# The statements of sixteen attention units in another order on four engines

## The chip, the cores and the metric

The kernel runs on one core of one Trainium2 chip. The metric is the device time of one execution in microseconds (us). The kernel before took 1912.51, 1914.97 and 1917.04 us in three runs; the median is 1914.97.

## The reference

For eight images of 256 x 256 and eight texts of 128 tokens the reference computes, in f32:

```
h  = edge image (grey, two Scharr convolutions, absolute values)   [8, 256, 256]
h  = concat(h, embedded bigram hashes of the text @ proj * scale)  [8, 384, 256]
h += block0(layernorm(h))   # LN, 16 heads of 16, rotary, causal softmax, Wo, LN, GELU MLP 256-1024-256, its own residuals
h += ffn(layernorm(h))      # ternary weights, relu, 256-1024-256
h += attn1(layernorm(h))    # 16 heads of 64 on 4 key heads, rotated queries, slopes * distance, causal,
                            # softmax with 1 added to the sum, Wo
h += experts(layernorm(h))  # router, top 2 of 8 experts, 960 slots each, silu(gate) * up, down, scatter add
```

Each image has 384 rows of 256 in three tiles of 128 rows. The weights' signs, the rotated query weights and the routing are computed in the kernel too.

## The kernel before, in words

After a setup there are sixteen attention units, one for each image and attention layer: units 0 to 7 are block0's attention of image u (layer 0), units 8 to 15 attn1's of image u-8 (layer 1). Then come the routing of tokens and the eight experts; the change touches neither.

A unit is made of one attention and of the dense work of other images that runs beside it. `Kind` says which: `s1` (lnA, queries and keys of the next image of layer 0, turned and stacked into high and low parts), `conv` (edges of the image two ahead), `s2` (output projection, MLP and ternary feed-forward of the image before), `s1p` (lnB, queries, keys and values for the next unit of layer 1), `s3` (output projection of layer 1, lnE and the router's logits). The units are U_FIRST, five U_MID0, U_SIX, U_SEVEN, U_EIGHT (the first of layer 1), six U_MID1 and U_LAST. In U_FIRST the `up0_` banks and the slots of `mlp_norm`, `mlp_rows` and `ffn_norm` carry the ternary weights and the rotated query weights instead. Each compute engine has a function `unit` with two lists of calls, one for each layer; the lists are written out by hand and the engine goes through its list strictly in order. The engines meet only in semaphores.

The attention of a unit has sixteen heads n in eight pairs p. TensorE computes `scores(p)` (causal, three row tiles) into banks 0 to 2. VectorE's `mask_max(n)` adds mask or slopes, writes `probs` (four buffers) and the row maxima (about three instructions and three reads). ScalarE's `exps(n)` takes the exponents with their sums. TensorE's `turn(n, 0)` and `turn(n, 1)` transpose half of the probabilities each, into bank 3 and bank 4. `take_turned(n)` copies bank 3 on ScalarE and bank 4 on VectorE. `mix(g)` multiplies four heads (layer 0) or two (layer 1) by the values into bank 5. `invert` (VectorE), `spread` (GpSimd), `divisors` (TensorE) and `take_divisors` (ScalarE) bring the reciprocal sums into columns, and `weigh` (VectorE) multiplies bank 5 with them, which frees it. `scores_ahead`, `mask_ahead` and the calls with `_last` belong to the seam with the next or the previous unit.

All dense products use banks 6 and 7 in turn. `dense_units` lists them in TensorE's order and `psum_plan` gives the k-th of them bank 6 + k % 2; a product waits until the last but one has been taken out of its bank (`banks.wait_free`). So the order of this list and of TensorE's calls must agree, and whoever takes a bank late holds up the second product behind it. A row-tile normalisation is three steps: `moments` on VectorE, `deviation` on GpSimd (the reciprocal root), the normalising instruction on VectorE; then TensorE transposes tile by tile (`lnA`, `lnB`, `lnM`, `lnF`, `lnE`). `rope(t)` on GpSimd rotates the queries and keys of tile t as soon as VectorE has taken them; ScalarE's `stack_upper(0)` waits for all three. SP's queue issues the loads and stores of each unit (text, images, spilled sums, `h_rows`, and after U_EIGHT the weights `wo1`); its order is in its own function and is not changed.

Lines: transposes of probabilities L982, of reciprocals L993, of normalised rows L918, scores L966, values products L1017, all products of `product` L1034, stacking L1056, down of the ternary layer L1194, exponents L1729, masking L2290, `take_turned` L1737 and L2433, normalising L2212, rotation L3165 to L3173.

Of the kernel before, what the change touches and what calls it, by code (L numbers as in the profile page):

```python
# [134 lines left out]
def dense_units(k):  # L135
# [6 lines left out]
    if k.layer == 0:  # L142
        add(k.tail is not None, "rinvT_tail")
        add(True, "v0_0", "v0_1")
        add(k.s2, "proj0_0", "proj0_1")
        add(True, "v0_2")
        add(k.s1, "lnA0", "lnA1")
        add(k.s2, "proj0_2")
        add(k.s1p, "lnB0", "lnB1", "q1_0")
        add(k.s1, "qk_0")  # L150
        add(k.conv, "conv0")
        add(k.s1p, "k1_0", "q1_2")
        add(k.conv, "conv1")
        add(k.s1, "qk_1", "qk_2")
        add(k.s2, "lnM0", "lnM1", "up0_0", "up0_1", "up0_2", "up0_3", "up0_4")
        add(k.s2, "up0_5")
        add(k.s1, "stk0_0_q")
        add(k.s2, "up0_6", "up0_7")
        add(k.s1p, "q1_3")
        add(k.s1, "stk0_0_k", "stk0_1_q")  # L160
        add(k.s2, "down0_0")
        add(k.s1, "stk0_1_k")
        add(True, "rinvT0")
        add(k.s1p, "q1_5")
        add(k.s1, "stk0_2_q", "stk0_2_k")
        add(k.s1p, "q1_1")
        add(k.s2, "down0_1", "down0_2")
        add(k.s1p, "q1_6", "q1_4", "q1_7", "k1_1")
# [4 lines left out]
        add(k.s2, "up1_1", "up1_2", "up1_3", "up1_4", "up1_5", "up1_6", "up1_7")  # L173
        add(k.s1, "stk1_1_q", "stk1_1_k")
        add(k.s2, "down1_0")
        add(k.s1, "stk1_2_q")
        add(k.s2, "down1_1", "down1_2")
        add(k.s1, "stk1_2_k")
    else:
        add(k.tail is not None, "rinvT_tail")  # L180
        add(True, "v1_0", "rinvT0")
        add(k.s3, "proj1_0")
        add(k.s2, "proj0_0", "proj0_1")
        add(k.s3, "proj1_1")
        add(True, "v1_1")
        add(k.s2, "proj0_2")
        add(True, "v1_2")
        add(k.s2, "lnM0", "lnM1")
# [3 lines left out]
        add(k.s1p, "lnB0", "lnB1", "q1_3")  # L192
        add(k.s2, "up0_2", "up0_3")
        add(k.s1p, "q1_0")
        add(True, "rinvT2")
        add(k.s2, "up0_4", "up0_5")
        add(k.s3, "lnE0", "lnE1")
        add(k.s2, "up0_6", "up0_7")
        add(True, "rinvT3")
        add(k.s2, "down0_0")  # L200
        add(k.s1p, "k1_0")
        add(True, "rinvT4")
        add(k.s2, "down0_1")
        add(k.s1p, "q1_5")
        add(k.s2, "down0_2")
        add(k.s1p, "q1_1", "k1_1", "q1_2")
        add(True, "rinvT5")
        add(k.s2, "lnF0", "lnF1", "up1_0", "up1_1")
        add(k.s1p, "q1_4")
        add(k.s2, "up1_2")  # L210
        add(k.s1p, "q1_6")
        add(True, "rinvT6")
        add(k.s2, "up1_3", "up1_4", "up1_5", "up1_6", "up1_7")
        add(k.s3, "logits")
        add(k.s1p, "q1_7")
        add(k.s2, "down1_0", "down1_1", "down1_2")
# [111 lines left out]
def early_fusion_kernel(nc, a, const, out):  # L328
# [23 lines left out]
    with ctx:  # L352
# [553 lines left out]
        def _(pe):  # L906
# [163 lines left out]
            def unit(sec, i, u, k):  # L1070
# [381 lines left out]
            k = banks.bank(SETUP, "txt_index")  # L1452
# [1936 lines left out]
```

## Time and profile before

| | |
|---|---|
| three runs | 1912.51, 1914.97, 1917.04 us |
| profiled execution, first to last instruction | 1913.2 us |
| instructions | 33649 |
| TensorE busy | 1771.8 us, 93% |
| VectorE busy | 1232.3 us, 64% |
| ScalarE busy | 968.2 us, 51% |
| GpSimd busy | 544.9 us, 28% |
| chain that ended last | TensorE 72%, issue 10%, VectorE 8% |
| HBM | 50 GB/s over the span |

The profile gives its execution's span only; the time of that same execution is not given apart from it, and the span lies between the lowest and the middle of the three runs. A busy share is an average over stages. The windows below cut the span at the units' seams: on TensorE a unit of layer 0 begins with `scores(1)`, one of layer 1 with `turn(0, 0)`. In a timeline row the bracket at the end is the idle time of the engine before that group and what ended it. Ends of matmuls are modelled, so the distance from one start to the next is the safer duration on TensorE.

### The profile page before, as it was taken

What the parts mean: (1) busy time and instruction counts of PE and PEld (TensorE: products, weight loads), DVE (VectorE), ACT (ScalarE), POOL (GpSimd) and SP (SyncE); (2) the same over time, 40 slices, a digit from 0 to 9 for tenths busy, and PEclk for the clock granted to TensorE, in tenths of its full rate; (3) what the DMA queues carried; (4) which work ended last, traced back from release to release, by engine and by line L of the source; (5) the groups of instructions that cost most, each with busy time, mean ns of one, the idle gap of its engine ahead of it and who ended that gap; (6) DMA issues with size and microseconds to landing.
All of it is one profiled execution on the core that took longest, in us unless ns stands there. A gap on an engine that the chain in (4) does not pass through costs nothing.

```text
span 1913.2 us, 33649 instructions
## 1 busy us (share of the span) xinstructions
PE 1771.8 (93%) x11231; PEld 1431.5 (75%) x11231; DVE 1232.3 (64%) x4073; ACT 968.2 (51%) x2669; POOL 544.9 (28%) x763
## 2 busy tenths in 40 slices
PE   5787999999999999899999999992999999999997
PEld 3455677776867677677887878862898998999896
DVE  6667677786867675756767777667854545454452
ACT  1355657575766766565576666640233334333421
POOL 2241434324242410111111111011425333533431
PEclk8687999999999999999999999996989999999998
DMA  6111010101101010103011110002222221222210
GB/s 209 39 37 62 3 62 1 62 1 61 36 11 59 1 34 1 34 1 94 1 35 34 34 34 2 26 26 85 86 75 92 99 71 40 82 79 67 64 40 21
DMA packets 74243, 91.03 MB, mean 48 GB/s; under 512 B 16523, under 2 KB 64310, under 8 KB 74072
## 3 DMA queue, kind: packets, MB, share of 16 engines
q1 hardware_dynamic: 61464, 67.90, 11.0%
q0 software_dynamic: 9472, 16.77, 3.2%
q10 hardware_dynamic: 3136, 4.21, 0.6%
q8 instruction: 91, 1.49, 0.3%
q14 instruction: 80, 0.66, 0.1%
HBM read 71.02 MB, written 25.00 MB: 50 GB/s over the span
## 4 chain that ended last, share of the span: by engine, by line
PE 72%; issue 10%; DVE 8%; POOL 2%; ACT 2%; DMA 2%; DVEq 1%; POOLq 1%; SPq 1%; ACTq 0%
PE bank L1605 16%; PE bank L1034 16%; PE bank L1620 9%; PE bank L982 6%; PE bank L1017 6%; PE bank L966 5%; PE bank L938 3%; PE bank L1194 2%; PE bank L1056 2%; PE bank L993 1%; PE bank L918 1%; PE bank L939 1%; DVE probs L2290 1%; DVE at_least L2913 1%; POOLq L3139 1%
## 5 line engine op out<-in xcount | busy, mean ns | idle before, releaser
L1729 ACT ACTIVATE probs<-probs,nmax 128x128 f32<-128x128 f32 (+2 forms) x768 | 381.1, 502 | 64.2 <-DVE nmax L2290 64.1
L982 PE MATMUL bank<-cst,probs 128*128 128x128 f32 x1536 | 234.9, 279 | 20.9 <-ACT probsT L1737 9.1
L982 PEld LDWEIGHTS bank<-cst,probs 128*128 128x128 f32 x1536 | 180.0, 142 | 53.9 <-issue 15.4
L1605 PE MATMUL bank<-xeT,gate_w 128*128 128x480 f32 x768 | 187.6, 379 | 0.5 <-issue 0.5
L1605 PE MATMUL bank<-xeT,up_w 128*128 128x480 f32 x768 | 187.1, 379 | 0.0
L2433 DVE COPY probsT<-bank 128x384 f32<-128x384 f32 x256 | 141.1, 551 | 65.1 <-PE bank L982 64.3
L1620 PE MATMUL bank<-down_w,hT 128*120 128x256 f32 x1536 | 181.3, 280 | 0.0
L1620 PEld LDWEIGHTS bank<-down_w,hT 128*120 128x120 f32 x1536 | 179.9, 181 | 0.1
L3076 DVE TENSOR_TENSOR prod<-bank,sil 128x480 f32<-128x480 f32 x128 | 84.1, 657 | 147.7 <-PE bank L1605 126.0
L3182 POOL COPY rinv<-rowsum 128x384 f32<-128x384 f32 x80 | 40.7, 509 | 480.7 <-DVE o1T L2312 289.9
L1737 ACT COPY probsT<-bank 128x384 f32<-128x384 f32 x256 | 121.8, 476 | 108.8 <-PE bank L982 100.0
L1650 ACT ACTIVATE sil<-bank 128x480 f32<-128x480 f32 x128 | 73.0, 571 | 175.8 <-PE bank L1605 161.9
L1605 PEld LDWEIGHTS bank<-xeT,up_w 128*128 128x128 f32 x768 | 145.0, 189 | 21.7 <-DVE up_w L3008 0.2
L1605 PEld LDWEIGHTS bank<-xeT,gate_w 128*128 128x128 f32 x768 | 144.3, 189 | 21.6 <-issue 0.6
L1729 ACT ACTIVATION_READ_ACCUMULATOR probs<-probs,nmax 128x1 f32 x768 | 147.6, 192 | 0.0
L2290 DVE CUSTOM_DVE_ANT_0 probs<-bank,alibi 128x128 f32<-128x128 f32 (+2 forms) x384 | 141.3, 420 | 1.9 <-issue 0.2
L3358 POOL DMA_INDIRECT out<-ye,slot_token x64 | 75.5, 1180 | 230.2 <-DVE ye L3089 218.3
L2290 DVE CUSTOM_DVE_ANT_0 probs<-bank,cst 128x128 f32<-128x128 f32 (+2 forms) x384 | 140.4, 420 | 0.7 <-issue 0.7
L966 PE MATMUL bank<-k1T,q1T 64*128 64x256 f32 (+2 forms) x768 | 100.5, 394 | 2.2 <-DVE nmax L2290 2.2
L1017 PE MATMUL bank<-probsT,v 128*64 128x384 f32 (+2 forms) x768 | 98.3, 392 | 0.0
L3328 POOL DMA_INDIRECT xe<-xn_rows,slot_token x64 | 71.2, 1112 | 93.1 <-DVEq L3014 52.7
L966 PEld LDWEIGHTS bank<-k1T,q1T 64*128 64x128 f32 x768 | 83.2, 186 | 17.9 <-issue 12.3
(350 smaller groups left out, 3420.3 us busy)
## 6 DMA issues: line engine op xcount, KB each, us to landing
gate_raw<-in_L_ffn_gate_w SPq DMA_DIRECT2D x8, 1024.0 KB
up_raw<-in_L_ffn_up_w SPq DMA_DIRECT2D x8, 1024.0 KB
down_raw<-in_L_ffn_down_w SPq DMA_DIRECT2D x8, 1024.0 KB, 5.7
img<-in_x SPq DMA_DIRECT2D x8, 768.0 KB
residual_rows<-x SPq DMA_DIRECT2D x8, 384.0 KB
residual_rows<-h_in SPq DMA_DIRECT2D x8, 384.0 KB
xr<-residual_rows SPq DMA_DIRECT2D x8, 384.0 KB, 4.4
hr<-residual_rows SPq DMA_DIRECT2D x8, 384.0 KB, 3.8
```

The costliest lines, as they stand in the source:

```text
L966: last = mm(scores_place(s, t), q[:, P * t:P * (t + 1)], k[:, 0:P * (t + 1)], start=True, stop=True)
L982: last = tr(ps[bank][:, P * q:P * (q + 1)], probs[:, n % 4, SEG[t] + P * j:SEG[t] + P * (j + 1)], ident)
L1017: last = mm(ps[5][rows_o, P * j:S], w, probsT[:, n % 4, cols_j], start=first, stop=final)
L1034: last = mm(ps[bank][:, 0:width], x, w, start=(k == 0), stop=(k == len(pieces) - 1))
L1605: last = mm(ps[bank][:, 0:HALF], w[:, wp, c, P * m:P * (m + 1)], xeT[:, xp, c, HALF * hf:HALF * (hf + 1)], start=(c == 0 and k == 0), stop ...
L1620: last = mm(ps[bank][:, D * (j % 2):D * (j % 2) + D][0:CP], hT[:, j // 4, hp, m, CP * (j % 4):CP * (j % 4 + 1)], down_w[:, wp, m, :], star ...
L1729: last = f(p, p, ACT.Exp, bias=nmax[:, n % 4, t:t + 1], scale=-1.0, accum_out=rowsum[:, where, t:t + 1])
L1737: nc.scalar.copy(probsT[:, n % 4, 0:3 * P], ps[3][:, 0:3 * P]).then_inc(freed[3], 1)
L2290: last = v.tensor_tensor_reduce(out=probs[:, n % 4, seg(t)], in0=scores_place(n, t), in1=bias[:, P * (2 - t):S], scale=1.0, scalar=BIG, op ...
L2433: v.tensor_copy(probsT[:, n % 4, 3 * P:6 * P], ps[4][:, 0:3 * P]).then_inc(freed[4], 1)
L3076: tt(prod[:, q % 2, :], k[:, 0:HALF], sil[:, q % 2, :], ALU.mult).then_inc(f_, 1)
L3358: g.indirect_dma_start(out_rows, slots(e, j), ye[0:CP, j, :], None, bounds_check=T - 1, oob_is_err=False).then_inc(scattered, 16)
```

## The change

The order of calls in the eight lists of `unit` on TensorE, ScalarE, VectorE and GpSimd (one for each layer on each engine) is changed, and `dense_units` with TensorE's. What each call does is the same. Banks 6 and 7 are given out anew by position, so some products change places between the two banks. The parts of the diff that the prediction speaks of, TensorE first:

```diff
 layer 0
                     scores(1)
                     mix_last()
+                    turn(0, 0)
                     divisors_last()
+                    turn(0, 1)
                     values(0)
-                    turn(0, 0)
-                    turn(0, 1)
+                    values(1)
+                    turn(1, 0)
+                    attn_rows(0)
+                    turn(1, 1)
                     scores(2)
-                    values(1)
-                    attn_rows(0)
-                    turn(1, 0)
-                    turn(1, 1)
+                    values(2)
                     attn_rows(1)
-                    values(2)
...
                     second_queries(0)
+                    second_keys(0)
                     queries_keys(0)
+                    queries_keys(1)
                     edges(0)
                     scores(3)
-                    second_keys(0)
                     second_queries(2)
+                    second_queries(3)
+                    queries_keys(2)
+                    turn(4, 0)
                     edges(1)
-                    queries_keys(1)
-                    queries_keys(2)
...
                     mlp_down(1)
                     mlp_down(2)
+                    second_queries(6)
                     turn(10, 0)
+                    second_queries(4)
+                    second_queries(7)
                     turn(10, 1)
-                    second_queries(6)
                     turn(11, 0)
-                    second_queries(4)
+                    norm_ffn()
                     scores(7)
-                    second_queries(7)
-                    second_keys(1)
-                    norm_ffn()
                     turn(11, 1)
-                    turn(12, 0)
                     stack(1, 0, "q")
                     ffn_up(0)
...
                     ffn_up(7)
-                    turn(14, 0)
+                    scores_ahead()
+                    ffn_down(0)
+                    stack(1, 1, "q")
                     turn(14, 1)
-                    stack(1, 1, "q")
-                    scores_ahead()
                     stack(1, 1, "k")
-                    ffn_down(0)
                     turn(15, 0)
+                    ffn_down(1)
+                    ffn_down(2)
                     stack(1, 2, "q")
                     turn(15, 1)
-                    ffn_down(1)
-                    ffn_down(2)
                     stack(1, 2, "k")
 layer 1
                     turn(0, 0)
                     scores(1)
-                    turn(0, 1)
                     mix_last()
                     divisors_last()
+                    values(0)
+                    turn(0, 1)
                     turn(1, 0)
-                    values(0)
                     scores(2)
...
+                    turn(4, 1)
+                    mlp_up(1)
                     mix(0)
...
                     scores(4)
...
                     turn(6, 1)
+                    mix(2)
                     scores(5)
...
+                    second_keys(0)
+                    mix(3)
                     scores(6)
...
                     ffn_up(6)
                     ffn_up(7)
-                    mix(6)
-                    turn(15, 1)
-                    router()
-                    second_queries(7)
                     ffn_down(0)
                     ffn_down(1)
                     ffn_down(2)
+                    divisors(6)
+                    mix(6)
+                    second_queries(7)
+                    turn(15, 1)
```

In layer 1, too, `scores_ahead()` has moved from in front of `turn(13, 1)` to behind `ffn_up(2)`, and `router()` from behind `turn(15, 1)` to in front of `turn(14, 1)`. On VectorE, layer 0 (a new place for `take_turned(0)` at the start, the layer norms of the edge image earlier, `take_turned(15)` behind the last two `ffn_rows`):

```diff
                     mask_max(3)
+                    take_turned(0)
                     weigh_last()
                     take_values(0)
+                    take_values(1)
                     gray_ahead()
-                    take_turned(0)
                     second_moments(0)
-                    take_values(1)
...
                     mlp_norm(0)
+                    mlp_norm(1)
+                    take_queries_keys(1)
                     mask_max(6)
                     edge_sum(0)
-                    mlp_norm(1)
                     first_moments(0)
-                    take_queries_keys(1)
+                    take_queries_keys(2)
+                    mlp_norm(2)
+                    first_norm(0)
+                    take_queries(3)
+                    attn_moments(0)
                     mask_max(7)
-                    mlp_norm(2)
-                    take_queries_keys(2)
+                    edge_sum(1)
```

On VectorE, layer 1, `mask_max(4)`, `take_turned(1)` and `attn_rows(0)`, `attn_rows(1)` now stand in front of `second_moments(0)`, which waits for a load of `h_in`. On ScalarE, layer 0, `exps(1)` stands in front of `take_turned(0)`, `exps(10)` and `exps(11)` around `stack_upper(1)` in front of `take_turned(9)`; at the end `exps(15)` stands in front of `take_stack(1, 1)` and `take_stack(1, 2)` stays last. In layer 1 its list ends with `take_turned(15)`, `take_divisors(6)` (before: `take_turned(15)`, `relu_of(6)`, `relu_of(7)`, with `take_divisors(6)` further up). On GpSimd, layer 0:

```diff
-                    rope(0)
                     deviation(LN_MLP, 1)
                     deviation(LN_MLP, 2)
+                    rope(0)
+                    rope(1)
                     deviation(LN_FIRST, 0)
-                    rope(1)
                     rope(2)
...
-                    ffn_residual()
                     deviation(LN_ATTN0, 2)
                     residual_x()
+                    ffn_residual()
                     residual_h()
```

## Rows read from the trace of the kernel before

**Rows 1.** Windows: stretch, length, busy time of each engine, clock, DMA.
```profile
115.00:175.00 60.00, 42.25 (x268) 29.09 (x267) 41.69 (x154) 35.12 (x111) 16.61 (x27) 0.74 0.00 1
349.10:434.40 85.30, 84.19 (x541) 63.37 (x540) 64.22 (x226) 54.98 (x160) 30.59 (x51) 1.00 0.11 35
605.70:690.30 84.60, 78.27 (x512) 58.42 (x510) 58.31 (x206) 55.41 (x161) 23.47 (x37) 0.98 0.09 29
690.30:769.50 79.20, 74.00 (x485) 56.56 (x485) 51.27 (x198) 51.30 (x153) 11.47 (x22) 0.98 0.07 21
769.50:866.30 96.80, 87.03 (x555) 66.72 (x554) 64.66 (x224) 57.53 (x157) 15.19 (x28) 0.98 0.06 17
866.30:927.90 61.60, 59.29 (x425) 47.04 (x424) 41.66 (x182) 38.27 (x129) 8.59 (x20) 1.00 0.25 73
927.90:987.00 59.10, 58.84 (x425) 47.01 (x424) 42.42 (x184) 38.17 (x129) 8.58 (x20) 1.00 0.09 28
```
**Rows 2.** TensorE's timeline in a layer-1 unit: start, duration, group.
```profile
963.26 0.82 PE L918 MATMUL bank<-cst,x_moe 128*128 128x128 f32 x6
963.91 0.82 PE L982 MATMUL bank<-cst,probs 128*128 128x128 f32 x6
964.66 1.52 PE L1017 MATMUL bank<-probsT,v 128*64 128x384 f32 x12
966.11 0.55 PE L993 MATMUL bank<-cst,rinv 128*128 128x128 f32 x3
...
977.20 1.52 PE L1017 MATMUL bank<-probsT,v 128*64 128x384 f32 x12
978.65 1.57 PE L966 MATMUL bank<-k1T,q1T 64*128 64x256 f32 x12
```
**Rows 3.** TensorE's timeline and one row of VectorE's in a layer-0 unit.
```profile
410.32 0.82 PE L982 MATMUL bank<-cst,probs 128*128 128x128 f32 x6
411.47 0.52 PE L982 MATMUL bank<-cst,probs 128*128 128x128 f32 x3 [0.33 <-ACT probsT L1737]
...
412.67 1.03 PE L918 MATMUL bank<-cst,xh_b 128*128 128x128 f32 x6
...
414.86 0.63 PE L1056 MATMUL bank<-ident_r,stk_q 128*128 128x128 f32 x4 [0.51 <-DVE x_parts L2543]
415.33 0.93 PE L1034 MATMUL bank<-x_parts,f1T 128*128 128x384 f32 x4
...
412.79 0.41 DVE L2212 TENSOR_SCALAR xh_b<-hr,mv_b,rstd_b 128x256 f32<-128x256 f32 x1 [0.31 <-POOL rstd_b L3140]
```
**Rows 4.** Timelines of the first unit; the last row groups GpSimd's over four layer-0 units.
```profile
132.62 1.11 PE L1156 MATMUL bank<-cst,tern_b 128*128 128x128 f32 x4 [3.90 <-ACT f1T L1648]
...
130.16 1.02 ACT L1693 CAST stk_q<-qk 128x256 fp32r<-128x256 f32 x3 [4.94 <-POOL qk L3173]
...
118.56 3.74 POOL L3165 TENSOR_TENSOR rot<-qk,cst 128x128 f32<-128x128 f32 x4 [3.22 <-DVE qk L2316]
...
L3165 POOL TENSOR_TENSOR rot<-qk,cst 128x128 f32<-128x128 f32 x48 | 20.7, 463 | 37.8 <-DVE qk L2316 37.2 <-issue 0.6
```
**Rows 5.** Timeline rows with the longer waits of the units at the joints.
```profile
624.76 0.79 PE L966 MATMUL bank<-k0T,q0T 64*128 64x256 f32 x6 [2.37 <-DVE nmax L2290]
...
706.42 0.42 PE L1034 MATMUL bank<-xs_hi,wq_hi 128*128 128x384 f32 x1 [2.10 <-DVE xs_lo L2580]
...
778.05 0.43 DVE L2205 BATCH_NORM_STATS2 stats_a<-h_in 128x6 f32<-128x256 f32 x1 [1.18 <-DMA h_in<-h_rows]
...
846.64 1.57 PE L966 MATMUL bank<-k1T,q1T 64*128 64x256 f32 x12 [1.83 <-DVE nmax L2290]
...
874.93 3.72 PE L1034 MATMUL bank<-wo,o1T 128*128 128x256 f32 x16 [1.55 <-DMA wo<-in_L_attn_Wo]
...
1272.29 0.84 PE L982 MATMUL bank<-cst,probs 128*128 128x128 f32 x6 [1.25 <-ACT probsT L1737]
```
**Rows 6.** The page's group of exponents: busy, mean ns, idle before.
```profile
L1729 ACT ACTIVATE probs<-probs,nmax 128x128 f32<-128x128 f32 (+2 forms) x768 | 381.1, 502 | 64.2 <-DVE nmax L2290 64.1
```

More of the change, by code:

```diff
@@ L1287, in unit @@
                     mlp_down(0)
-                    stack(0, 1, "k")
-                    mix(1)
                     divisors(0)
@@ L1292, in unit @@
                     turn(8, 1)
-                    second_queries(5)
+                    stack(0, 1, "k")
+                    mix(1)
                     stack(0, 2, "q")
                     stack(0, 2, "k")
+                    second_queries(5)
+                    second_queries(1)
                     turn(9, 0)
-                    second_queries(1)
                     turn(9, 1)
@@ L1354, in unit @@
+                    turn(2, 1)
                     second_rows(1)
-                    turn(2, 1)
+                    turn(3, 0)
                     values(1)
-                    attn_rows(2)
-                    turn(3, 0)
                     scores(3)
+                    norm_mlp()
+                    turn(3, 1)
+                    turn(4, 0)
                     values(2)
-                    turn(3, 1)
-                    norm_mlp()
                     second_rows(2)
+                    mlp_up(0)
@@ L1420, in unit @@
[L1420 to L1426 removed]
+                    ffn_up(0)
+                    second_queries(4)
+                    turn(13, 1)
+                    turn(14, 0)
+                    ffn_up(1)
+                    ffn_up(2)
+                    scores_ahead()
                     second_queries(6)
[L1428 removed]
@@ L1429, in unit @@
                     ffn_up(3)
                     ffn_up(4)
+                    router()
+                    turn(14, 1)
                     ffn_up(5)
@@ L2713, in unit @@
                     weigh_last()
+                    take_values(0)
                     take_turned(0)
-                    take_values(0)
+                    mask_max(4)
+                    take_turned(1)
+                    attn_rows(0)
+                    attn_rows(1)
                     second_moments(0)
-                    mask_max(4)
                     second_moments(1)
-                    attn_rows(0)
-                    moe_rows(0)
-                    take_turned(1)
-                    attn_rows(1)
@@ L2761, in unit @@
-                    take_moe()
+                    mlp_rows(0)
                     take_turned(9)
-                    invert(4)
-                    mlp_rows(0)
                     weigh(3)
                     mask_max(12)
+                    invert(4)
+                    invert(5)
+                    take_turned(10)
+                    take_queries(5)
+                    mask_max(13)
                     ffn_norm(0)
-                    take_turned(10)
-                    invert(5)
```

347 lines of the change are left out of this document (163 added, 184 removed).

## The prediction

> **What bounds the kernel now.** I read the busy table and the 40 slices first. TensorE is busy 93% of the span, VectorE 64%, ScalarE 51%, GpSimd 28%, so TensorE's own stream is the length wherever it has no gap. The change touches only the sixteen attention units; in the trace they end at 1276 us, and from there to 1913 us nothing moves. I then cut the windows at the units' seams [rows 1]. The reader is to see three kinds of unit. A steady layer-1 unit (927.9 to 987.0) has 58.84 us of TensorE in 59.10, and a steady layer-0 unit (349.1 to 434.4) has 84.19 in 85.30: there the order on the other engines can only do harm, and an order on TensorE can only win what its own switches cost. The units at the joints have gaps: 17.75 us in the last 60 us of the first unit (115 to 175), 6.3 in the next-to-last layer-0 unit that still feeds layer 0 (605.7), 5.2 in the one after it, 9.8 in the first layer-1 unit (769.5), 2.3 in the second. Last I read TensorE's timeline by the statement, for where each gap stands and what released it.
>
> **The change, part by part.** No instruction is added or removed, so each term is a gap closed, a gap opened, or a switch saved. I laid the new TensorE list end to end with start-to-start durations of the rows and, beside it, the new lists of ScalarE and VectorE, and asked of each statement when its input is there.
>
> *Steady layer-1 units.* Six transposes take 0.65 us (963.26 to 963.91), but 0.75 when a values product follows; the product takes 1.45 before a transpose (964.66 to 966.11) and also 1.45 before scores (977.20 to 978.65) [rows 2]. So going into the narrow matmuls (scores or values product, 64 rows or columns of the array) costs 0.10 us, and passing from one narrow kind to the other costs nothing; coming out I take at 0.05, an estimate from the same rows (the three transposes of 966.11 take 0.48 with an entry behind them, against 0.325 + 0.10). An island costs 0.15. The list of before has 15 islands in such a unit, the new one 12: mix_last, mix(0), mix(2) and mix(3) now touch a scores group, and the pair mix(5), scores_ahead is parted. That is 3 x 0.15 = 0.45 us per unit. All inputs are there by my walk; the closest are the exponents of head 0 of the next unit, about 0.2 us before its first transposes, and the bank of the lnE transposes. Six such units: -2.7 us. Bounds: 0 (exit cost nothing, one small wait anew) to -4.
>
> *Steady layer-0 units.* No island is won (11 and 11). Before, the stretch after the last mlp_down runs 410.32, a wait of 0.33 at turn(11, 0), scores(7), the transposes lnF at 412.67, and a wait of 0.51 at 414.86 for the split of their result; ffn_up(0) starts at 415.33 [rows 3]. The last of the three row tiles is normalised only at 412.79, after GpSimd's deviation [rows 3], 2.47 us behind 410.32. The new list takes scores(7) out from in front of lnF: lnF is reached 0.75 us sooner, at 1.5 us behind that mark, and its last two transposes then wait about 0.85 us for the same normalisation. scores(7) then fills the time in which the split is made, so the 0.51 shrinks to nothing. Net about +0.1; the stall at turn(11, 0) stays. Earlier in the unit the divided transposes and two values() push attn_rows(0) on VectorE behind the grey image, which I price at +0.2 (a bank and turn(3, 1) late). So +0.3 per unit, five units: +1.5 us. Bounds: -2.5 (all gaps of the row gone, 5 x 0.5) and +6 (the lnF wait whole, in six units with the one at 605.7).
>
> *The first unit, 115 to 175.* TensorE waits 3.90 us at 132.62 for a bank that ScalarE frees; ScalarE had waited 4.94 us until 130.16 for the last rotation on GpSimd, and GpSimd began its second rotation only at 118.56, because queries_keys(1) stood behind both edge products [rows 4]. The new list has queries_keys(1) right behind queries_keys(0) and the third between the edges, so GpSimd does the first two rotations in a row. By the mean of rows 4, four small multiplies 1.85 us, a rotation is 4.6 us; the last one then ends near 124 rather than 130. Behind it come new waits: first_norm(0) and the moments now stand before mask_max(7), which I find 2 us later than before; scores(4) waits some 0.5. What follows is bound by VectorE, busy 41.69 of the 60 us [rows 1]. I take -3.0 us, nearest to the 3.90 of that wait, of which the rest of the queue gives some back. Bounds: +1 and -7.
>
> A page of the Trainium skill speaks against part of this: *SBUF — State Buffer*, section "Who interferes with whom", has VectorE and GpSimd share one port pair, as an exclusive lock, and counts a tensor_tensor with both inputs in SBUF among what contends. The trace agrees in kind: the four multiplies take 3.74 us beside the weight work of VectorE and 1.85 elsewhere. By that rule the second rotation, now started beside the two 2048-wide comparisons of the weights, would be held up and the first unit would give about 0 instead of -3.
>
> *Units at the joints* [rows 5]. At 624.76 TensorE waits 2.37 us for mask_max(5): the new list puts a second queries_keys (1.8 us) in front of scores(3): -2.0. At 706.42 it waits 2.10 for the split of lnB; the chain is the same, but two more transposed groups are reached sooner, second_keys and a better lnF: -1.0. In the unit at 769.5, VectorE stands 1.18 us behind a DMA of h_in (778.05) with mask_max(4) queued behind it; the new list takes mask_max(4), take_turned(1) and two attn_rows first. At 846.64 scores_ahead waits 1.83 for mask_max(13..15); it now stands two ffn_up later. Of 9.8 us of gaps I take back 2.0: against it stands that ffn_down(0) follows ffn_up(7) at once, where before 2.4 us of other work lay. The wait of 1.55 us at 874.93 for the wo1 weights goes: ffn_down ends 2.5 us earlier in its unit, so h_rows is stored and wo1 loaded earlier: -1.8 with the small one beside it. In the last unit router() moves into the wait of 1.25 us at 1272.29: -1.2. Together -8.0, bounds -14 and 0.
>
> *What I can't see.* Each engine's queue is in order, and I walked some 100 statements on three of them; waits of 0.1 to 0.3 us will be missed. I add +1.5 (0.1 per unit); bounds 0 and +5. SP's queue is not reordered; the spills it waits for come earlier, since residual_x and residual_h no longer wait for the last attn_norm near the seam.
>
> Sum: -2.7 + 1.5 - 3.0 - 8.0 + 1.5 = -10.7 us. Against the profiled execution, span 1913.2, that is 1902.5; the median of the three runs lies 1.8 above that span, so 1914.97 - 10.7 = 1904.3, and I say 1904.
>
> **Rivals.** *More comes back (0.20).* The first unit and the joints give their bounds: TensorE's clock is granted at 0.74 of full speed (between its levels 1.2 and 2.4 GHz) over 115 to 175 [rows 1], after the gaps; fewer gaps may keep the higher level there. With -7 and -12 in place of -3 and -8 the sum is -18.7: 1896. For it: the gaps are 41 us in all. Against: VectorE's queue behind the first gap.
> *Nothing measurable (0.14).* The gaps move but are not closed: a joint waits elsewhere in the same chain. Then layer 1's -2.7, layer 0's +1.5 and the unseen waits are left, about -1: 1914. For it: the chain at 706.42 is latency, not order.
> *The seam is late (0.12): slower.* In layer 0 stack(1, 2, "q") has moved behind ffn_down(2), and ScalarE's take of it stands before exps(0) of the next unit, whose exponents were ready before the seam and now run across it; in layer 1 rinvT6's copy stands before exps(0) with 0.2 us to spare. If one more head's exponents are in front than I placed, each seam loses one exps, 3 x 0.502 = 1.5 us [rows 6]; 12 seams are +18 on -10.7: 1922. It decides from 0.9 us per seam. For it: in-order queues and small slack in six units; against: in layer 0 I find 0.8 us of slack.
> *The change does not act:* the units of layer 1 are full of TensorE work, so equal time there is likely, but the orders do differ on all engines; I give it no share.
>
> **How the numbers follow.** My forecast 0.54, the rivals 0.20, 0.14, 0.12. What a measurement can tell from no change is 0.2%, 3.8 us: faster means under 1911.1. Forecast and first rival are faster in nearly all of their spread (0.72 of 0.74), the rest of them and the second rival are same (0.15), the third slower and a little of the second (0.13). The likeliest case alone reaches from 1898 to 1911. For 8 in 10 I go to 1894 below, past most of the first rival, and 1915 above, which takes in the second; outside are the seam case and the tail of the first.
>
> **What would show it.** Layer-1 period: 58.5 to 58.7 us instead of 59.05; a period over 59.3 with turn(0, 0) waiting for ScalarE's probs is the seam rival. Layer-0 period 85.4 to 85.8 with a gap inside lnF, released by xh_b, and none at ffn_up(0). First unit: the wait of ScalarE for qk gone, TensorE's 3.90 gone, seam at 172 instead of 175. Joints: no 2.37 at scores(3), no wo1 wait. I am wrong if the layer-0 units lose more than 1 us each, or if the seam of the first unit does not come earlier.

## The result and the profile after

The changed kernel takes 1881.51 us (median of 4 runs, 1877.40 to 1883.02) against 1913.74 before (4 runs, 1912.31 to 1917.04): ratio 0.982, 95% interval 0.980 to 0.984. That is 32 us less, where I had forecast 10.7; the range ended at 1894. The profiled executions span 1880.0 and 1913.2 us, 33.2 apart.

The windows of the kernel after, cut as those of [rows 1] at the first statement of each unit (columns: stretch, length, busy time of TensorE, its weight loads, VectorE, ScalarE, GpSimd, granted clock, DMA):

```profile
109.50:169.50 60.00, 44.43 (x302) 31.34 (x301) 47.52 (x174) 35.07 (x110) 25.78 (x36) 0.89 0.13 44
341.60:427.60 86.00, 83.93 (x541) 62.99 (x540) 67.16 (x226) 54.94 (x161) 31.07 (x51) 1.00 0.11 35
599.80:679.40 79.60, 75.76 (x509) 57.67 (x508) 58.27 (x206) 55.55 (x162) 23.61 (x37) 1.00 0.10 31
679.40:755.80 76.40, 71.97 (x486) 55.98 (x486) 52.02 (x197) 50.99 (x155) 11.54 (x22) 1.00 0.07 22
755.80:846.70 90.90, 84.13 (x555) 65.60 (x554) 62.85 (x227) 57.89 (x159) 14.97 (x28) 1.00 0.07 23
846.70:904.80 58.10, 58.10 (x425) 47.20 (x424) 43.07 (x185) 38.17 (x131) 8.37 (x20) 1.00 0.25 71
904.80:962.90 58.10, 58.10 (x426) 47.20 (x424) 43.06 (x185) 38.17 (x131) 8.40 (x20) 1.00 0.09 29
1195.30:1266.00 70.70, 69.47 (x488) 55.47 (x487) 48.20 (x196) 34.21 (x118) 9.00 (x21) 1.00 0.08 25
```

Put beside [rows 1], line by line: the seam of the first unit comes 5.5 us earlier (169.5 against 175.0), and the clock in its last 60 us is 0.89 instead of 0.74. The steady layer-0 unit is longer, 86.0 against 85.3. The three units at the joints are 5.0, 2.8 and 5.9 us shorter, and in each of them the clock is 1.00 where it was 0.98. The second layer-1 unit is 3.5 shorter, the steady one 1.0, and neither has an idle moment left. The last line is the last unit with the tail of the attention, which took 75.3 before. Where the time came from, beside what the prediction had for it (us):

| stretch | forecast | profiles |
|---|---|---|
| first unit, to its seam | -3.0 | -5.5 |
| five steady layer-0 units | +1.5 | -0.4 (the first of them -2.7, the others +2.3) |
| units at 605.7, 690.3, 769.5 | -5.0 | -13.7 |
| second layer-1 unit | -2.25 | -3.5 |
| five steady layer-1 units | -2.25 | -4.8 |
| last unit | -1.2 | -4.6 |
| not seen | +1.5 | |
| behind the attention, where nothing changed | 0 | -0.7 (613.1 to 617.1 us long in the 14 profiles of this case) |
| sum | -10.7 | -33.2 |

The clock's part can be read directly. In the kernel before, each of four joints has one stretch at half speed; the windows are cut on them:

```profile
626.00:629.40 3.40, 3.40 (x5) 1.33 (x4) 3.40 (x8) 3.40 (x14) 3.26 (x4) 0.51 0.00 0
707.90:711.30 3.40, 3.40 (x19) 2.30 (x20) 2.38 (x14) 2.25 (x9) 0.00 (x0) 0.50 0.01 2
783.00:786.40 3.40, 3.40 (x13) 2.65 (x11) 3.04 (x13) 0.62 (x4) 1.93 (x5) 0.50 0.00 0
1274.50:1277.90 3.40, 3.40 (x17) 1.74 (x16) 0.00 (x0) 0.48 (x1) 0.00 (x0) 0.50 0.00 0
```

TensorE is busy through all of each at 1.2 GHz instead of 2.4, so each holds 1.7 us of work less than at full clock; what that costs the unit is measured below. They begin 1.2 us behind the end of the wait of 2.37 at 624.76, 1.5 behind that of 2.10 at 706.42, 0.2 behind one of 2.34 at 782.78 and 2.2 behind that of 1.25 at 1272.29 [rows 5]. The profile after has none between 163 and 1268 us.

### The profile page after: what moved, and what is told of

Its sections match the earlier page's. It is cut to its first block, busy times and chain, and to the rows that moved or that the text cites. A ratio compares the mean times of both kernels' runs of the same rounds, so it can differ in the third digit from the quotient of the medians.

```text
span 1880.0 us, 33649 instructions
## 1 busy us (share of the span) xinstructions
PE 1751.2 (93%) x11231; PEld 1427.0 (76%) x11231; DVE 1248.4 (66%) x4073; ACT 967.2 (51%) x2669; POOL 545.7 (29%) x763
## 4 chain that ended last, share of the span: by engine, by line
PE 75%; issue 9%; DVE 7%; POOL 3%; ACT 2%; DVEq 2%; POOLq 1%; DMA 1%; SPq 0%; ACTq 0%
PE bank L1601 17%; PE bank L1030 16%; PE bank L1616 10%; PE bank L978 7%; PE bank L962 6%; PE bank L1013 6%; PE bank L1190 3%; PE bank L934 2%; PE bank L1052 2%; PE bank L989 1%; PE bank L914 1%; PE bank L935 1%; DVE at_least L2909 1%; POOL rstd_b L3136 1%; PE bank L1582 1%
```

## The experiments

Each hybrid keeps both sets of lists and picks one by the kind of the unit, on all four engines and in `dense_units`, banks included.

**One layer at a time: e1_layer1, e2_layer0.**

```
NEW_ORDER = (U_EIGHT, U_MID1, U_LAST)              # e1_layer1
NEW_ORDER = (U_FIRST, U_MID0, U_SIX, U_SEVEN)      # e2_layer0
if k in NEW_ORDER: ...lists of the changed kernel
else: ...lists of before
```

> New order for the layer-1 units alone (the unit behind the joint, six steady ones, the last); layer 0 as before. Theory A (each unit's gain is its own): the units give what they gave in the whole change, 5.9 + 3.5 + 4.8 + 4.6 = -18.8 us, so about 1895 us, steady layer-1 period 58.1 us, no fall of the granted clock from the unit at the joint on. Rival B (a unit's gain depends on how the unit before it ends): the first new unit loses at its seam with the old order and the sum is -13 or less, above 1900 us.

> New order for the eight layer-0 units alone; layer 1 as before. Theory A: the rest of the change, -33 + 18.8 = -14 us, so about 1899.5 us; steady layer-0 period 86.06 us (slower than before by 0.7), first unit about 9 us shorter, steady layer-1 period 59.05 as before. Rival B: not the rest; the two parts then add up to less or more than -33 by over 3 us.

e1_layer1: 1893.80 us, ratio 0.9895 (0.9873 to 0.9917), -20.2 against 1914.01 of the shared runs of before. e2_layer0: 1898.94, ratio 0.9929 (0.9907 to 0.9951), -15.1. Together -35.3, the whole change -32.2; each is known to some 4 us either way, so the parts add up. A steady layer-1 unit of e1_layer1 is the one of the changed kernel, whatever stands ahead of it:

```profile
1096.80:1154.90 58.10, 58.10 (x425) 47.23 (x424) 43.10 (x185) 38.10 (x131) 8.38 (x20) 1.00 0.10 28
```

Theory A holds, rival B falls. More than half of the gain is layer 1's, where my terms came to -7.7 us (2.0, 2.25, 2.25 and 1.2 in the table): e1_layer1 gave 20.2. Layer 0's terms came to -4.5, and e2_layer0 gave 15.1.

**The first unit: e4_first and e7_rope.** e4_first has `NEW_ORDER = (U_FIRST,)`. e7_rope has the old lists in the first unit too, but for this:

```
 queries_keys(0)
+queries_keys(1)
 edges(0)
 ...
-edges(1)
-queries_keys(1)
 queries_keys(2)
+edges(1)
# GpSimd: rope(0), rope(1), deviation(LN_FIRST, 0), rope(2)
# VectorE: take_queries_keys(1) ahead of mask_max(6), (2) ahead of mask_max(7)
```

> New order for the first unit alone. Theory A: it gives 9 to 11 us by itself, about 1904 us: some 3.4 us of TensorE's gaps and the rest the granted clock, whose half-speed stretches in and around this unit shrink from 46 to 30 us. Rival D (the stretches of half clock fell otherwise by chance, as the setup ahead of the unit, whose order is unchanged, also shows other stretches in the two traces): only the gaps are gained, 3 to 4 us, about 1910 us, with half-speed stretches as long as before.

> The kernel before with one part of the new order, in the first unit alone: queries_keys(1) right behind queries_keys(0), the third between the two edge products, VectorE's takes with them, and GpSimd's first two rotations in a row. Theory A (the rotation chain is what held this unit): it gives most of the 9.4 us that the whole new order of this unit gave, 6 us or more, time 1908 or less, TensorE's wait of 3.90 gone. Rival S (the rest of the new order does it, above all the normalisations that stand earlier): 3 us or less, about 1911, the wait goes but comes back at the stacks or at scores(4).

e4_first: 1904.63, ratio 0.9950 (0.9934 to 0.9965), -9.4 us: as theory A had it. e7_rope: 1910.08, ratio 0.9977 (0.9967 to 0.9988), -4.3 us: between the two theories. By these medians the rotation is a bit under half of e4_first's gain, but the intervals (2.3 to 6.3 us and 6.7 to 12.6) leave its share open. By the profiles it is more: from the first transposes of the first unit to those of the third e7_rope takes 164.7 us and e4_first 162.6, the six profiles with the old first unit 169.2 to 171.9. The waits of e7_rope (start, duration, group, idle before and its releaser):

```profile
127.53 0.79 PE L1044 MATMUL bank<-k0T,q0T 64*128 64x256 f32 x6 [0.95 <-DVE nmax L2721]
...
150.23 0.88 PE L1060 MATMUL bank<-cst,probs 128*128 128x128 f32 x3 [3.68 <-ACT probsT L2026]
```

and of the changed kernel:

```profile
126.44 0.80 PE L962 MATMUL bank<-k0T,q0T 64*128 64x256 f32 x6 [2.93 <-DVE nmax L2286]
...
133.12 0.80 PE L962 MATMUL bank<-k0T,q0T 64*128 64x256 f32 x6 [2.35 <-DVE nmax L2286]
...
149.71 1.51 PE L978 MATMUL bank<-cst,probs 128*128 128x128 f32 x6 [3.69 <-ACT probsT L1733]
```

The 3.90 of [rows 4] is gone from both. In the changed kernel it comes back in part at two scores, behind row maxima on VectorE (5.3 us, where I had 0.5 for one of them), and TensorE's gaps in the last 60 us fall only from 17.75 to 15.57. The rotations do run in a row, but the last one ends at 129.2, not near 124 (130.1 before):

```profile
118.31 3.46 POOL L3166 TENSOR_TENSOR qk<-qk,cst 128x256 f32<-128x256 f32 x2
...
127.90 1.27 POOL L3169 TENSOR_TENSOR qk<-qk,rot 128x512 f32<-128x512 f32 x1
...
118.86 2.32 DVE L2172 TENSOR_TENSOR tern_b<-tern_b,f_raw 128x2048 f32<-128x2048 f32 x1
```

ScalarE starts to stack the rotated rows at 129.95, where it was 130.16 before. It doesn't wait for them any more because it is itself late: its exponents wait for row maxima until 126.37. So in the changed kernel the 3.90 is for the most part moved to the scores, and not won. In e7_rope the last rotation ends at 126.1 and the stacking starts at 126.12. What I had no term for is the clock. From its first transposes to those of the next unit the first unit takes 82.2 to 83.6 us in the six profiles with its old order, 27.6 to 37.9 of them at half speed, 77.6 with 24.8 in e7_rope, and 73.5 to 77.2 with 17.5 to 25.7 in six with the new order (which where it stands in the unit behind reaches these transposes 1.1 us sooner). The 77.2 is e4_first's own, so by this measure the two hybrids hardly differ. The unit behind takes 87.1 us in e7_rope and 85.4 in e4_first, but behind an old first unit it takes anything from 85.6 to 88.4. Which statement carries the rest was not tried.

**The fall of the clock behind a wait: e6_fill, e12_fill_fits.** The kernel before with products that only fill the wait of 2.37 us, 20 of them in e6_fill and 9 in e12_fill_fits:

```
+def fill(sec, i, name, n):
+    banks.wait_free(pe, sec, name, i)
+    for _ in range(n):
+        mm(ps[banks.bank(sec, name)][:, 0:P], ident, ident, start=True, stop=True)
+if k is U_SIX:
+    fill(sec, i, "qk_1", n)
 scores(3)
```

> The kernel before with 20 idle-time products of the identity (0.109 us each, 2.2 us; their result is overwritten) on TensorE in front of scores(3) of the next-to-last layer-0 unit, in its wait of 2.37 us. Nothing ends earlier by itself. Theory K (the half-speed stretch of 3.4 us at 626, right behind that wait, is caused by it): no half-speed stretch in this unit, which takes 82.9 us instead of 84.5. Rival L (the clock there falls for another reason): the stretch stays and the unit takes 84.5 or more.

> The kernel before with 9 products of the identity in front of scores(3) of the next-to-last layer-0 unit (they took 0.23 us each with 20 of them, so 2.1 us: inside the wait of 2.37). Theory K (a half-speed stretch follows a long wait of TensorE): no half-speed stretch behind it, eight products of queries_keys in 3.7 us instead of 5.4, and the unit takes 82.9 us instead of 84.5, with more work in it. Rival L: 84.5.

The products take 0.23 us each, twice what I had assumed, so e6_fill overran the wait by 2.2 us; e12_fill_fits repeats it with the right size. TensorE in the kernel before:

```profile
624.76 0.79 PE L966 MATMUL bank<-k0T,q0T 64*128 64x256 f32 x6 [2.37 <-DVE nmax L2290]
625.48 5.40 PE L1034 MATMUL bank<-wqkv,xTa 128*128 128x512 f32 x8
```

and in e12_fill_fits:

```profile
621.13 2.17 PE L930 MATMUL bank<-cst 128*128 128x128 f32 x18
623.66 0.79 PE L971 MATMUL bank<-k0T,q0T 64*128 64x256 f32 x6 [0.36 <-DVE nmax L2297]
624.38 3.70 PE L1039 MATMUL bank<-wqkv,xTa 128*128 128x512 f32 x8
628.01 1.50 PE L1022 MATMUL bank<-probsT,vpad 128*32 128x384 f32 x24
630.43 0.30 PE L918 MATMUL bank<-cst,xh_b 128*128 128x128 f32 x1 [0.91 <-DVE qk L2323]
632.53 1.20 PE L918 MATMUL bank<-cst,xh_b 128*128 128x128 f32 x5 [1.80 <-DVE qk L2323]
```

The same eight products behind the scores take 3.70 us instead of 5.40 (e6_fill: 3.70 too). That the filling did this is not shown by it, for e9_join, which fills nothing and has the old lists in layer 0, has the wait of 2.37 us and then 3.70 as well:

```profile
626.25 0.79 PE L966 MATMUL bank<-k0T,q0T 64*128 64x256 f32 x6 [2.37 <-DVE nmax L2290]
626.98 3.70 PE L1034 MATMUL bank<-wqkv,xTa 128*128 128x512 f32 x8
630.61 1.50 PE L1017 MATMUL bank<-probsT,vpad 128*32 128x384 f32 x24
633.00 0.30 PE L918 MATMUL bank<-cst,xh_b 128*128 128x128 f32 x1 [0.90 <-DVE qk L2316]
635.10 0.77 PE L918 MATMUL bank<-cst,xh_b 128*128 128x128 f32 x5 [1.79 <-DVE qk L2316]
```

Without filling the half-speed stretch stands right behind this wait in five of six profiles, with filling in neither of two. Theory K is the likelier one, and not shown by these two runs. Its 82.9 us for the unit is missed: 85.4 here, and 85.0 in e6_fill, which has no fall in this unit and 2.2 us too much in it. In e12_fill_fits the stretch is there after all, as rival L has it, but later, at 632.7: the transposes of xh_b, which waited 1.05 us before, now wait 2.71, and it begins behind this second wait, as it does at 636.1 in e9_join:

```profile
624.38:628.00 3.62, 3.62 (x10) 1.44 (x8) 3.41 (x9) 3.62 (x15) 3.34 (x4) 1.00 0.00 0
632.70:636.10 3.40, 3.40 (x15) 2.56 (x15) 0.68 (x1) 2.36 (x7) 3.10 (x5) 0.50 0.03 7
```

Here the fall behind the 2.37 costs nothing by itself. From the start of scores(3) to the last five transposes of xh_b it is 8.86 us with it (before) and 8.85 without it (e9_join; e12_fill_fits 8.87), since these transposes wait for VectorE's take of qk, which doesn't come sooner. The unit at 690.3 has no such cover. Taken from its first transposes to those of the next unit, it is, in the new order, 74.1 us without a fall (three profiles), 75.6 with one (two) and 77.0 with two (one); in the old order 75.7 to 75.8 with one (six). So a fall is 1.5 us there, and the new order with the fall only 0.2 better than the old one with it. In the last unit, up to its last transposes of x_moe, the old order takes 73.1 to 73.2 with a fall and 71.5 without, 1.6 us; in the first layer-1 unit the new one takes 91.4 to 91.6 with and 90.9 without, 0.5 to 0.7.

Over the 14 profiles of this case, a fall beyond the first unit stands in joints alone. With the old order the unit at 605.7 has one in 6 of 6 unfilled, that at 690.3 in 8 of 8, that at 769.5 in 8 of 8 (some have two or three), the one behind it in 4 of 8, the last one in 4 of 8. With the new order it is 0 of 6, 3 of 6, 3 of 5, 0 of 5 and 0 of 5 (e8_parted, which changes layer 1, left out of the last three). That is what ties the falls to the order. What ties them to waits is their place: each of these 44 falls began between 0.4 us ahead of and 2.2 us behind the end of a wait of TensorE of 1.2 to 2.9 us. Of the 23 waits of 2.0 us and more, 21 have one there, of the 66 waits of 1.2 to 2.0 us only 23. The steady units of all kernels, with no wait over 1.2 us once they run evenly, have none. So the same lists give a fall in one profile and none in another; the changed kernel's own profile happens to show none at all.

**The steady layer-0 units: e3_mid0_old, e5_residual_late.** e3_mid0_old leaves U_MID0 alone out of `NEW_ORDER`. e5_residual_late is the changed kernel with

```
 # VectorE                        # GpSimd
 ffn_lower(1)                    +ffn_residual()
-attn_norm(2)                     deviation(LN_ATTN0, 2)
 ...                              residual_x()
 take_stack(1, 1)                -ffn_residual()
+attn_norm(2)                     residual_h()
```

> The changed kernel with the five steady layer-0 units put back in the old order (first, next-to-last and last layer-0 unit and all of layer 1 new). Theory A: the new order loses 0.7 us in each steady layer-0 unit, so this one is 3.4 us faster than the changed kernel, about 1878 us, with periods of 85.36. Rival C: the new order of the steady units is what feeds the units around them (their seams and the clock), so that the three neighbours lose 1 us or more each and the time is 1881 or above.

> The changed kernel with one thing put back in layer 0: the third normalisation of the next sequence stands late again on VectorE, and GpSimd's sums residual_x and residual_h, which wait for it, stand behind ffn_residual. Theory P (in the changed kernel VectorE's cast of relu takes 1.99 us instead of 0.35 because residual_h runs on GpSimd at that moment; TensorE's new wait of 0.86 at ffn_up follows from it): the long cast is 0.36 again, the wait of 0.86 is gone, the steady layer-0 period is 85.2 instead of 86.06, about 1877.5 us. Rival Q (the wait comes from ScalarE's relu standing behind other work in the new order): the wait stays, period 86.0, time unchanged at 1881.5.

e3_mid0_old: 1879.28, ratio 0.9828 (0.9805 to 0.9851), 2.2 us under the changed kernel, which ran in another job (0.9822, 0.9802 to 0.9842, so the two intervals overlap). Its five steady units take 4.2 us less than the changed kernel's, as theory A has it, but its profile has two falls of the clock at the joints (695.2, 770.3) and is 2.7 us longer there; whether that is C or chance this run doesn't tell. Chance is enough for it: with all of layer 0 new, the unit at 690.3 has no fall in the changed kernel and in e2_layer0 and one in e8_parted. e5_residual_late: 1878.21, ratio 0.9811 (0.9797 to 0.9824), 3.3 under the changed kernel with overlapping intervals again; what is clear of noise is its steady period, 84.98 instead of 86.07 from the second of these units on. The changed kernel on VectorE and GpSimd:

```profile
411.14 0.89 DVE L2549 TENSOR_TENSOR hid_parts<-relu,hid_parts 128x384 fp32r<-128x384 f32 x1
411.96 1.99 DVE L2547 CAST hid_parts<-relu 128x384 fp32r<-128x384 f32 x1
...
409.78 1.83 POOL L3227 TENSOR_TENSOR xr<-hr,rows 128x768 f32<-128x768 f32 x1 [0.16 <-issue]
411.58 2.15 POOL L3216 TENSOR_TENSOR h_in<-h_in,rows 128x768 f32<-128x768 f32 x1
```

The cast starts at 411.96 and ends at 413.95, just behind GpSimd's addition (413.73); ScalarE's relu waits for it, and TensorE waits for that:

```profile
405.49 0.44 PE L914 MATMUL bank<-cst,xh_b 128*128 128x128 f32 x2 [0.75 <-DVE xh_b L2208]
...
415.25 0.97 PE L1030 MATMUL bank<-x_parts,f1T 128*128 128x384 f32 x4 [0.86 <-ACT relu L1646]
```

In e5_residual_late the addition runs later, the same cast takes 0.36 us, and the wait at 415.25 has no counterpart:

```profile
409.94 0.36 DVE L2547 CAST hid_parts<-relu 128x384 fp32r<-128x384 f32 x1 [0.22 <-ACT relu L1646]
...
422.94 1.83 POOL L3216 TENSOR_TENSOR h_in<-h_in,rows 128x768 f32<-128x768 f32 x1
```

In the changed kernel the five casts of this line that overlap the addition take 1.99 us each, and the 26 that overlap no large addition on GpSimd all stay under 0.7; in e5_residual_late none overlaps it and none is longer than 0.81. P is shown, Q falls, though the run moves the third normalisation too. The Trainium skill has this in *SBUF — State Buffer*, section "Who interferes with whom": a cast on VectorE can enter a mode that takes the port pair shared with GpSimd, and then whoever holds the pair blocks the other for its whole instruction. The trace agrees (1.99 us against 0.36).

**What layer 1's 0.98 us per unit is made of: e8_parted, e9_join, e10_q3.** An island is a run of narrow products (scores or values) with full-width ones on both sides.

```
# e8_parted, on the changed kernel          # e9_join, on the kernel before
 mix(0)                                     -mix(3)
+turn(5, 0)                                  divisors(3)
 scores(4)                                   mlp_down(0)
 # and scores(5) behind divisors(2),        +mix(3)
 # scores(6) behind turn(10, 0)              scores(6)
# e10_q3, on the kernel before: second_queries(3) from behind scores(5) to behind turn(7, 0)
```

> The changed kernel with three of the joined pairs of narrow products in layer 1 parted again (mix and scores with transposes or the divisors between them), so 15 islands instead of 12 in a steady unit. Theory of the prediction (0.15 us an island): period 58.09 + 0.45 = 58.54. Rival (only the entry into a narrow product costs, 0.09 us): 58.37. Rival (islands cost nothing, the gain of 0.98 per unit is made of small waits): 58.09.

> The kernel before with one swap in layer 1 on TensorE: divisors(3) ahead of mix(3), so that mix(3) and scores(6) touch in a steady unit (14 islands of narrow products instead of 15). Theory (an island costs 0.15 us: 0.10 going in, 0.05 coming out): steady period 59.06 - 0.15 = 58.91. Rival (0.19 to 0.23, as the unit of the kernel with three islands parted had beside its waits): 58.85. Rival (order of narrow products costs nothing): 59.06. A new wait at mix(3) or divisors(3), if there is one, stands in the trace and is taken off.

> The kernel before with second_queries(3) of layer 1 behind turn(7, 0), as in the new order, instead of right behind scores(5). Theory W (the idle 0.23 us in each steady layer-1 unit is the wait of this product for the split of its input, not the engine's own issue time): the gap goes and the period falls from 59.06 to 58.8 or less, 6 x 0.23 = 1.4 us over the steady units. Rival (it is issue time of the product behind scores): the gap stays and the period too.

e8_parted: period 60.67, +2.58. Two waits of 1.9 us together opened with the parting, and the 0.68 beside them is more than three islands at 0.15; the islands' price can't be read cleanly from it:

```profile
996.25 0.52 PE L978 MATMUL bank<-cst,probs 128*128 128x128 f32 x3 [0.73 <-ACT probsT L1733]
...
1004.60 0.52 PE L989 MATMUL bank<-cst,rinv 128*128 128x128 f32 x3 [1.17 <-DVE xs_lo L2576]
```

e9_join: period 59.87, slower by 0.81, not faster. The divisors, drawn ahead, meet a bank that ScalarE has not emptied:

```profile
969.41 0.52 PE L993 MATMUL bank<-cst,rinv 128*128 128x128 f32 x3 [0.78 <-ACT xTb L1648]
969.86 1.52 PE L1017 MATMUL bank<-probsT,v 128*64 128x384 f32 x12
971.31 1.57 PE L966 MATMUL bank<-k1T,q1T 64*128 64x256 f32 x12
972.81 0.55 PE L982 MATMUL bank<-cst,probs 128*128 128x128 f32 x3
```

With only these 0.78 us taken off, as the expectation has it, the period is 59.09, as if the island were worth nothing. But start to start the six transposes in front of the divisors take 1.60 us where they take 0.66 without a wait, so the delay is 0.94, and without it the period is 58.93. Taken start to start over the whole unit, the entries into narrow products sum to 1.30 us for 14 instead of 1.40 for 15, and the slower second transpose behind an island (0.165 instead of 0.109, 56 ns) falls away once: 0.13 us for one island, near the 0.15. Going from one narrow kind to the other costs as much as coming out (0.20 for the last product in both cases), so only the entry and the tail are saved. It would be noise beside a single misplaced wait. e10_q3 moved one product, and the idle 0.23 us of the kernel before is gone:

```profile
957.62 1.57 PE L966 MATMUL bank<-k1T,q1T 64*128 64x256 f32 x12
959.12 0.55 PE L982 MATMUL bank<-cst,probs 128*128 128x128 f32 x3
959.42 0.42 PE L1034 MATMUL bank<-xs_hi,wq_hi 128*128 128x384 f32 x1
```

Its period is 58.74, -0.33 (before: 957.10, then 958.90 with 0.23 idle ahead). The split of the product's input on VectorE stood there all along:

```profile
957.77 1.02 DVE L2580 TENSOR_TENSOR xs_lo<-bank,xs_hi 128x384 fp32r<-128x384 f32 x2 [1.33 <-ACT xs_hi L1803]
```

It ends at 958.79 and the product starts 0.11 us later; in e10_q3 it ends at 959.31 and the product starts at 959.42, again 0.11 later, with three transposes in between. So theory W holds, though the profile called that idle time "issue". Three islands (0.4), this (0.33) and a third small wait that the changed kernel doesn't have, 0.19 us ahead of the divisors at 982.45, make 0.92 of the 0.98.

**The best version: e11_best.** The lists of e5_residual_late in U_MID0, the changed kernel's elsewhere.

> The changed kernel with the late residual sums and the late third normalisation in the five steady layer-0 units alone (the first unit keeps the changed order). By the traces: first steady unit 85.0 instead of 86.8, the others 84.97, the rest as in the changed kernel: 5 x 1.09 = 5.4 us less than 1881.5, about 1876. Rival (the half-speed stretches at the joints, which came back in both kernels that were faster in these units, eat it): 1878 to 1880.

1876.42 us (5 runs, 1874.03 to 1877.42), ratio to before 0.9796 (0.9779 to 0.9813); 5 us under the changed kernel, whose runs are of another job; the intervals just overlap, but the five steady units are 84.96 to 85.01 us long instead of 86.05 to 86.09, which is 5.4 us, as expected. One fall of the clock is left, in the unit at the layers' joint:

```profile
253.30:338.30 85.00, 83.79 (x542) 63.07 (x540) 65.50 (x226) 55.04 (x161) 30.91 (x52) 1.00 0.11 35
593.20:673.20 80.00, 76.08 (x510) 57.71 (x509) 58.36 (x206) 55.64 (x162) 23.81 (x38) 1.00 0.10 33
673.20:749.60 76.40, 71.94 (x486) 55.95 (x485) 52.04 (x197) 50.97 (x154) 11.53 (x22) 1.00 0.07 22
749.60:841.00 91.40, 84.97 (x556) 67.03 (x555) 63.13 (x227) 57.93 (x160) 14.97 (x28) 0.98 0.07 23
```

## Why the prediction was wrong

The sign was right and the size a third. Step by step:

- *Steady layer-1 units, -0.45 each:* mis-sized, -0.98. The islands are near what I said. The term left out the idle 0.23 that [rows 1] show (58.84 busy in 59.10): I had it before me as "issue" and took it for the engine's own. It was a wait (e10_q3), with 0.10 of restart behind it, and 0.19 more stood ahead of the divisors. The sentence that an order "can only win what its own switches cost" there is the step that failed in layer 1.
- *Steady layer-0 units, +0.3 each:* the mechanism I named came as named (the wait inside lnF, 0.75 for the 0.85, released by xh_b; the 0.33 stays, the 0.51 gone), and the period is +0.7. What I missed is residual_h against the cast, 0.86; in e5_residual_late, without it, the period is 0.4 us under the old one, where I had +0.3 over it. I had written of the residual sums only that they come earlier, and of the port rule only in the first unit. It was the right rule and bore on both places, but I priced it in one: in the first unit, too, one multiply of the second rotation takes 2.77 us (median of its line 0.73), beside the 2048-wide product of the weights and not beside the two comparisons. The unit gave 5.5 us all the same, and not about 0.
- *First unit, -3.0:* TensorE's gaps in the last 60 us give 2.2 and the unit 5.5 by its seam, 9.4 by the time of e4_first. The last rotation ended at 129.2 where I had it near 124: the three took 6.4, 6.9 and 5.0 us instead of 4.6 each. The row maxima behind it cost 5.3 us instead of 0.5. The term had no clock in it: from the first transposes of the unit to those of the next, 34.5 us were at half speed before and 17.5 after, 8.5 us of work. At 0.74 of full speed the work that stands there costs more than it should, and that share is won along with the gaps.
- *Joints, -8.0:* the gaps named closed as named: no 2.37 at scores(3), no DMA wait for wo1, the wait at 706.42 shorter (1.56), that of the router gone. From [rows 1] and the windows after, TensorE's idle time falls by 2.5, 0.8 and 3.0 us in the three units and by 2.3 in the second layer-1 unit; in the last one, by the timeline, from 3.4 to 1.0. That is 11 us for the 8. These units gave 21.8, past my bound of 14. Some 1 us in each of the three layer-1 units is what the steady ones gave too. The rest is work that ran at half speed before and at full speed after, 4 x 1.7 = 6.8 us by the busy time. By the length of units with and without a fall, three of the four falls cost 1.5, 0.5 to 0.7 and 1.6 us; the one at 626.0 cost nothing up to the transposes of xh_b, and what it cost behind them no run isolates. At 690.3 the gap that I priced at 1.0 is worth some 0.2, the fall 1.5.
- *Unseen waits, +1.5:* the one that counts was not small: the 0.86 behind the cast, 4.3 us over the five steady layer-0 units. The first steady layer-0 unit lost the waits that it had inherited (88.7 to 86.0).

So the failing step is the price of a wait: the -3.0 and the -8.0 price each gap at its own length, with no clock in them, and the -2.7 counts no small waits. I spoke of the clock only in the rival "more comes back", as something that might hold in the first unit. In this kernel a wait of TensorE of 2 us and more was in 21 of 23 cases accompanied by 3.4 us or more at half speed, worth 0.5 to 1.6 us beyond the wait itself where units with and without it can be compared. That the wait brings the clock down is the likely reading of where the falls stand; the runs that filled a wait don't isolate it. The rival had the right mechanism and place; its time, 1896, was still too slow, because it took 12 us for the joints, less than even their bound of 14, where they gave 21.8, and it kept layer 1's -2.7 without the small waits. "Nothing measurable" was summed wrong: -2.7, +1.5 and the unseen +1.5 make +0.3, not -1, so its time was 1915 and not 1914; nothing else hangs on it. "The seam is late" did not happen: no steady layer-1 unit has a wait, and probs of the next unit are in time.

What stays open: which statements beyond the rotation's give the rest of the first unit, what decides whether a wait of 1.2 to 2.4 us has a fall behind it (the same lists do both), and whether the new places in banks 6 and 7 did anything by themselves, since every hybrid took banks and order together.

## What to carry to other kernels

Before pricing a gap of TensorE, read the granted clock in the microseconds behind it: a wait that is followed by a half-speed stretch can be worth its length and up to half that stretch, less where TensorE would next wait for another engine anyway. Before a missing stretch is taken as proof of what removed it, look through the profiles in which nothing was changed there: here one of six lacked it too. An idle time that is put down to "issue" and comes back in every round at the same place can be a wait; move the instruction once and see. When a statement moves on one engine, ask for each large GpSimd operation that it releases what VectorE casts or copies at that moment.

## What the runs showed of the hardware

- A fall of TensorE's clock to 1.2 GHz lasted 3.4 us or twice that at the joints, and each of the 44 beyond the first unit began between 0.4 us ahead of and 2.2 us behind the end of a wait of 1.2 to 2.9 us. Not every such wait had one: 21 of 23 of 2.0 us and more, 23 of 66 of 1.2 to 2.0 us.
- The same lists of a unit took 74.1 us without a fall, 75.6 with one and 77.0 with two; where TensorE next waited for VectorE, a fall added nothing (8.86 us against 8.85).
- A cast of 128x384 on VectorE took 1.99 us instead of 0.36 beside a 128x768 addition on GpSimd.
- A product of the 128x128 identity in f32 took 0.23 us and is recorded as two instructions, a transpose of the same size 0.11.
- Going from full-width products into narrow ones cost 0.09 us at the last product in front (0.202 instead of 0.109) and 0.06 behind (0.165 instead of 0.109) (first of the transposes behind). The last values product took 0.20 both in front of transposes and in front of scores.
